# A graph layer pair on one core: four-tile chunks between the two edge passes

## What is computed

```python
# layer 0
h_mean = segment_sum(x[src], dst) / maximum(deg, 1)
out1   = batch_norm(x @ W_self1 + h_mean @ W_neigh1)          # over the nodes
h_max  = where(deg > 0, segment_max(relu(x @ W_pool + b_pool)[src], dst), 0)
out2   = batch_norm(x @ W_self2 + h_max @ W_neigh2)
x1     = layernorm(x + leaky_relu(out1 + out2, 0.01))         # over the features
# layer 1: 8 heads of 12
Q, K, V = x1 @ Wq + bq, x1 @ Wk + bk, x1 @ Wv + bv
score  = exp(clip(sum(K[src] * Q[dst] / sqrt(12) * (edge_attr @ We + be), heads), -5, 5))
out    = layernorm(x1 + segment_sum(V[src] * score, dst) / (segment_sum(score, dst) + 1e-6))
```

## Time and profile before

| | us |
|---|---|
| median of 3 runs | 4208.73 (4200.21 to 4212.95) |
| the profiled execution | 4194.81 |
| its span, first to last instruction | 4193.1 |

### The profile page before, as it was taken

How to read it: one execution, slowest core, us unless ns; L and a number is a source line. 1 busy time by engine, 2 the same in 40 slices (tenths; PEclk the granted TensorE clock), 3 DMA queues, 4 the chain that set the end, 5 groups by cost and what they waited for, 6 DMA issues and landing times.

```text
span 4193.1 us, 106504 instructions
## 1 busy us (share of the span) xinstructions
PE 3764.5 (90%) x30408; PEld 3251.6 (78%) x30408; DVE 2323.7 (55%) x5891; ACT 1500.0 (36%) x4201; POOL 3080.6 (73%) x3253
## 2 busy tenths in 40 slices
PE   7988888888888888888899999999999999999996
PEld 6777777777777777777678888888888888888885
DVE  6555555555555555555645555555555555555556
ACT  3333333333333333333433333333333333333333
POOL 7777777777777777777367777777777777777774
PEclk9999999999999999999889999999999999999997
DMA  3111111111111111111134444444444444444442
GB/s 92 40 39 39 39 39 39 39 39 39 39 39 39 39 39 39 39 39 39 41 114 120 118 118 118 118 118 118 118 118 118 117 118 117 119 117 118 118 118 74
DMA packets 208678, 330.89 MB, mean 79 GB/s; under 512 B 72878, under 2 KB 156521, under 8 KB 208649
## 3 DMA queue, kind: packets, MB, share of 16 engines
q0 software_dynamic: 129040, 238.05, 23.0%
q1 hardware_dynamic: 79608, 92.48, 7.5%
HBM read 323.08 MB, written 7.22 MB: 79 GB/s over the span
## 4 chain that ended last, share of the span: by engine, by line
POOL 42%; issue 33%; DMA 10%; PE 9%; DVE 5%; POOLq 1%; ACT 1%; DVEq 0%; ACTq 0%; SPq 0%
POOL kvg L413 42%; DMA kvg<-kv_table,idx 8%; DMA kvg<-in_x_dram,idx 2%; DVE prod L927 1%; DVE msg L951 1%; PE bank L1206 1%; PE bank L1041 1%; PE bank L1220 1%; PE bank L1052 1%; PE bank L1237 1%; PE bank L1215 1%; PE bank L1101 1%; PE bank L1084 1%; DVE S L661 1%; POOLq L408 0%
## 5 line engine op out<-in xcount | busy, mean ns | idle before, releaser
L413 POOL DMA_INDIRECT kvg<-kv_table,idx x1613 | 1525.3, 946 | 508.6 <-issue 465.0
L413 POOL DMA_INDIRECT kvg<-in_x_dram,idx x1613 | 1527.3, 947 | 496.9 <-issue 487.1
L678 DVE TENSOR_TENSOR_SCAN scan<-keepC,scan,bank 96x512 f32<-96x512 bf16 x404 | 515.4, 1276 | 493.9 <-PE bank L1052 489.6
L1041 PE MATMUL bank<-ident,kvg 128*96 128x128 f32 x3232 | 450.7, 283 | 225.6 <-DMA kvg<-in_x_dram,idx 215.7
L1041 PEld LDWEIGHTS bank<-ident,kvg 128*96 128x96 f32 x3232 | 365.7, 164 | 290.0 <-DMA kvg<-in_x_dram,idx 217.6
L1206 PE MATMUL bank<-ident,S 128*64 128x128 f32 x3232 | 433.6, 278 | 135.6 <-DVE S L661 133.2
L920 DVE TENSOR_TENSOR prod<-kvg,bank 128x384 f32<-128x384 f32 x404 | 223.8, 554 | 578.6 <-DMA kvg<-kv_table,idx 430.6
L1206 PEld LDWEIGHTS bank<-ident,S 128*64 128x64 f32 x3232 | 345.4, 137 | 224.2 <-issue 224.2
L1101 PEld LDWEIGHTS bank<-S,scanE 128*96 128x96 f32 x3232 | 340.4, 166 | 217.9 <-issue 214.7
L492 ACT COPY scanE<-bank 128x384 f32<-128x384 f32 x404 | 193.3, 478 | 753.1 <-PE bank L1093 753.1
L1220 PE MATMUL bank<-qwin,scan 64*128 64x96 f32 x3232 | 458.7, 283 | 0.0
(11 more groups left out here) (155 smaller groups left out, 5102.4 us busy)
## 6 DMA issues: line engine op xcount, KB each, us to landing
ea<-in_edge_attr_dram SPq DMA_DIRECT2D x402, 192.0 KB
kvg<-in_x_dram,idx POOLq DMA_INDIRECT x1613, 2.5
kvg<-kv_table,idx POOLq DMA_INDIRECT x1613
kv_table<-stage SPq DMA_DIRECT2D x6, 672.0 KB, 3.3
xN<-in_x_dram SPq DMA_DIRECT2D x6, 336.0 KB, 3.1
out_dram<-xN SPq DMA_DIRECT2D x6, 336.0 KB
src_all<-in_src_groups_dram SPq DMA_DIRECT2D x1, 804.0 KB
stage<-in_dst_groups_dram SPq DMA_DIRECT2D x1, 804.0 KB
```

The costliest lines, as they stand in the source:

```text
L413: pool.indirect_dma_start(out=to[:, r, j, :], out_offset=None, in_=table, in_offset=bass.IndirectOffsetOnAxis(ap=idx[:, r, j:j + 1], axis= ...
L678: dve.tensor_tensor_scan(out=scan[:, r % 2, :], data0=keepC[:, r % 2, :], data1=bank[2 + r % 2][0:D, :], initial=scan[:, (r + 1) % 2, GE - ...
L1041: pe.matmul(bank[0][0:D, j:GE:J], xg[:, r, j, 0:D], ident[:, :], start=True, stop=True)
```

## The change

Constants: LATE 3 to 2, so 99 strips and 112 rest columns; chunks of Q = 4 tiles, 13 of them, the last of one tile; HEAD = 12 turns.

- **Strips.** The four groups of a turn now do: count and reciprocal; mean; branch 1; branch 2 (before: count; reciprocal with branch 2; mean; branch 1).
- **Batch-norm statistics.** The statistics of the first 96 strips are aggregated ahead: branch 1 after turn 99, branch 2 after turn 100, on DVE between the turns (`gathered_stats`). What is left for later are 27 numbers a branch.
- **Rest columns.** Their count, reciprocal and mean move into the drain of pass 1 (`rest_out`), and so does the load of the flag.
- **Chunks.** Scaling and adding both branches is done by PE with two diagonal weight matrices; ACT makes the two parts of the leaky slope from PSUM, POOL adds them and then adds xT.
- **Table.** K and V are computed from the rows before normalising, with weights centred over the features (`w_kvc`), and DVE scales by the reciprocal deviation and adds the bias (`b_kv`) on the way to `stage`. It no longer waits for the normalised rows.
- **Turning back.** The normalised tiles are turned to `xT` one per group in the first 12 turns of pass 2 (PE, then DVE in `queries`), only the first tile before it; ACT clears `acc` one tile per group instead of POOL's one memset. ACT's `window(r)` waits for `s_qc` of group r - 1.
- **Warming.** Six pairs ahead of the chunks instead of nine; none within the chunks and in pass 2.

The diff, cut to its core:

```diff
-LATE = 3
+LATE = 2
+FLAG_TURN = 4
+NA = TURNS - LATE - 3
+Q = 4
+NQ = -(-NT // Q)
+HEAD = 12
...
+        def two_parts(eng, turn, lag, peel=0):
+            peel = max(peel, -(-lag // R))
+            for p in range(peel):
+                turn(p, range(R), lambda r: p * R + r >= 0, True)
+            if peel < HEAD:
+                with eng.Fori(peel, HEAD) as i:
+                    turn(i, range(R), lambda r: True, True)
+            with eng.Fori(HEAD, TURNS) as i:
+                turn(i, range(R), lambda r: True, False)
+            turn(TURNS, range(lag), lambda r: r < 0, False)
...
@@ sync (SP)
+            for k in range(NQ):
+                n = len(tiles_of(k))
+                sp.wait_ge(s_kvD, k + 1)
+                sp.dma_start(kv_table[k * Q * P:(k * Q + n) * P, :].rearrange("(t p) c -> p t c", p=P),
+                             stage[:, k * Q:k * Q + n, :]).then_inc(s_kvtab, 16)
...
@@ gpsimd (POOL)
+            for k in range(NQ + 1):
+                if k < NQ:
+                    u = acc[0:D, 1, columns(k)]
+                    pool.wait_ge(s_l, k + 1)
+                    pool.tensor_tensor(u, u, scan[:, k % 2, 0:u.shape[1]], ALU.add).then_inc(s_leak, 1)
+                if k >= 1:
+                    at = columns(k - 1)
+                    pool.wait_ge(s_leak, k)
+                    pool.tensor_tensor(acc[0:D, 0, at], acc[0:D, 1, at], xT[0:D, at], ALU.add).then_inc(s_h, 1)
-            pool.wait_ge(s_hN, NK)
-            pool.memset(acc[:, 0, :], 0.0).then_inc(s_free0, 1)
...
@@ scalar (ACT)
+            for k in range(NQ + 2):
+                if k < NQ:
+                    at = columns(k)
+                    act.wait_ge(s_u, k + 1)
+                    z = bank[k % 2][0:D, 0:at.stop - at.start]
+                    wait_past(act, s_leak, k - 1)
+                    act.activation(scan[:, k % 2, 0:at.stop - at.start], z, ACT.Identity, bias=shs[:, 1:2], scale=0.01)
+                    act.activation(acc[0:D, 1, at], z, ACT.Relu, bias=shs[:, 0:1], scale=0.99).then_inc(s_l, 1)
+                if k >= 2:
+                    t = k - 2
...
+                    act.wait_ge(s_mv, t + 1)
+                    act.activation(qr[b][:, 0:n], qmv[b].rearrange("p (n c) -> p n c", c=2)[:, 0:n, 1], ACT.Sqrt,
+                                   bias=eps_col[:, 0:1]).then_inc(s_sd, 1)
+                    act.wait_ge(s_nb, t + 1)
+                    for j in tiles_of(t):
+                        last = act.activation(xN[:, t * Q + j, :], bank[2 + b][:, j * D:(j + 1) * D], ACT.Identity,
+                                              bias=qb[b][:, j:j + 1], scale=qr[b][:, j:j + 1])
+                    last.then_inc(s_x1, 1)
...
                 def window(r):
+                    act.wait_ge(s_qc, freed(i, r, 1))
                     act.wait_ge(s_q, freed(i, r, 2))
...
@@ vector (DVE)
+                def rest_out():
+                    dve.wait_ge(s_countR, 1)
+                    dve.tensor_scalar_max(share_rest, bank[6][0:D, W:W + REST], 1.0).then_inc(s_shareR, 1)
...
+                    if isinstance(i, int) and i == TURNS and r == 1:
+                        rest_out()
+                        held["flag"] = load_flag(dve)
...
+            def gathered_stats(m, done, n):
+                part = stats[:, m, NA - 1, :]
+                dve.bn_aggr(mv[:, m, :], stats[:, m, 0:NA, :].rearrange("p n c -> p (n c)")).then_inc(done, 1)
...
+            pipeline(dve, turn1, 4, peel=XTURNS + 1, between=(count_descents, count_outside, count_early, centring),
+                     ending=(lambda: gathered_stats(0, s_part, 0), lambda: gathered_stats(1, s_part, 2)))
...
+            for k in range(NQ + 1):
+                if k < NQ:
...
+                    for j in tiles_of(k):
+                        last = dve.bn_stats(st[:, j, :], bank[2 + b][:, j * D:(j + 1) * D])
...
+                        last = dve.bn_aggr(mean_var[:, j, :], st[:, j, :])
...
+                if k >= 1:
+                    t = k - 1
+                    dve.wait_ge(s_kv, t + 1)
+                    for j in tiles_of(t):
+                        last = dve.scalar_tensor_tensor(
+                            out=stage[:, t * Q + j, :],
+                            in0=bank[4 + t % 2 * 2 + j // 2][:, j % 2 * 2 * D:(j % 2 + 1) * 2 * D],
+                            scalar=qr[t % 2][:, j:j + 1], in1=b_kv[:, :], op0=ALU.mult, op1=ALU.add)
+                    last.then_inc(s_kvD, 1)
+                if k < NQ:
+                    dve.wait_ge(s_sd, k + 1)
+                    dve.reciprocal(qr[b][:, 0:n], qr[b][:, 0:n]).then_inc(s_rs, 1)
+                    dve.wait_ge(s_rs, k + 1)
+                    dve.scalar_tensor_tensor(out=qb[b][:, 0:n], in0=mean_var[:, 0:n, 0], scalar=-1.0,
+                                             in1=qr[b][:, 0:n], op0=ALU.mult, op1=ALU.mult).then_inc(s_nb, 1)
...
@@ tensor (PE)
+                    if isinstance(i, int) and i == TURNS and r == 1:
+                        pe.wait_ge(s_acc, NG + AHEAD)
+                        pe.matmul(bank[6][0:D, W:W + REST], pick[:, :], acc[0:DSUM, 0, rest], start=True, stop=True
+                                  ).then_inc(s_countR, 1)
+                        held["flag"] = load_flag(pe)
...
-            stay_warm(9, 7)
+            for _ in range(6):
+                pe.matmul(bank[7][:, 0:CH], ident[0:D, :], xT[0:D, 0:CH], start=True, stop=True)
+            pe.wait_ge(s_diag, 2)
+            for k in range(NQ + 2):
+                if k < NQ:
...
+                    pe.matmul(o, diag[:, 0, :], acc[0:D, 0, at], start=True, stop=False)
+                    pe.matmul(o, diag[:, 1, :], acc[0:D, 1, at], start=False, stop=True).then_inc(s_u, 1)
+                if k >= 2:
+                    t = k - 2
+                    b = t % 2
+                    pe.wait_ge(s_h, t + 1)
+                    wait_past(pe, s_x1, t - 1)
+                    for j in tiles_of(t):
+                        last = pe.transpose(bank[2 + b][:, j * D:(j + 1) * D],
+                                            acc[0:D, 0, (t * Q + j) * P:(t * Q + j + 1) * P], ident[0:D, 0:D])
+                    last.then_inc(s_hN, 1)
+                    wait_past(pe, s_kvD, t - 1)
+                    pe.wait_ge(s_wkc, 1)
+                    for j in tiles_of(t):
+                        last = pe.matmul(bank[4 + b * 2 + j // 2][:, j % 2 * 2 * D:(j % 2 + 1) * 2 * D],
+                                         acc[0:D, 0, (t * Q + j) * P:(t * Q + j + 1) * P], w_kvc[:, :],
+                                         start=True, stop=True)
+                    last.then_inc(s_kv, 1)
...
-            pipeline(pe, turn2, 3)
+            two_parts(pe, turn2, 3, peel=HEAD)
```

More of the change, by code:

```diff
@@ L228, in wait_past, with pipeline @@
                 eng.wait_ge(s, value)
-        def pipeline(eng, turn, lag, turns=TURNS, per=R, peel=0, between=()):
+        def pipeline(eng, turn, lag, turns=TURNS, per=R, peel=0, between=(), ending=()):
             peel = max(peel, -(-lag // per))
@@ L238, in pipeline, with tiles_of, columns @@
                     work()
-            if peel < turns:
-                with eng.Fori(peel, turns) as i:
+            last = turns - len(ending)
+            if peel < last:
+                with eng.Fori(peel, last) as i:
                     turn(i, range(per), lambda r: True)
+            for p in range(last, turns):
+                turn(p, range(per), lambda r: True)
+                ending[p - last]()
             turn(turns, range(lag), lambda r: r < 0)
-        def node_rows(t, k):
-            return bank[t % 2 * 2 + k // 4][:, (k % 4) * D:(k % 4 + 1) * D]
+        def two_parts(eng, turn, lag, peel=0):
[8 more added lines that the diff above has]
+            turn(TURNS, range(lag), lambda r: r < 0, False)
+        def tiles_of(k):
+            return range(min(Q, NT - k * Q))
+        def columns(k):
+            return slice(k * Q * P, min((k + 1) * Q, NT) * P)
         def own_tiles(i, r):
@@ L461, in _, with clear @@
             last_residual()
+        def clear(act, at):
+            act.copy(acc[0:DMSG, 0, at], eps_col[0:DMSG, 1:2].to_broadcast([DMSG, P]))
         def copy_indices(act, i, r, s_done, s_i):
@@ L472, in _ @@
             act.wait_ge(s_ones, 2)
-            act.copy(warm[:, :], ones_col[0:1, :])
+            act.activation(warm[:, :], ones_col[0:1, :], ACT.Sqrt)
             act.wait_ge(s_src, 48)
@@ L508, in _ @@
             act.wait_ge(s_bn, 1)
             act.activation(std[:, :], mv[:, :, 1], ACT.Sqrt, bias=eps_col[0:D, 0:1]).then_inc(s_std, 1)
+            act.copy(acc[0:D, 1, rest], bank[0][0:D, 0:REST]).then_inc(s_copyR, 1)
             act.wait_ge(s_z, 1)
[L511 to L531 removed]
@@ L757, in _ @@
             dve.wait_ge(s_scan, NG + AHEAD)
-            with irregular(dve):
+            with dve.If(held["flag"] > 0):
                 with dve.Fori(0, NCH) as c:
@@ L1117, in turn1 @@
                         back(r - 2)
```

(17 more changed lines are left out.)

326 lines of the change are left out of this document (150 added, 176 removed).

## The result

The changed kernel took a median of 4214.68 us (4206.38 to 4226.14, 20 runs) against 4205.72 us for the kernel before (4200.21 to 4218.31, 20 runs, the three shown above among them): a ratio of 1.0019, 95% interval 1.0012 to 1.0026, so 8.0 us more (5.0 to 10.9). The profiled execution has a span of 4206.7 us, 13.6 more than the one before.

The account below looks back on a forecast made before the run. POOL's gathers bound both passes, so only its 91.9 us gap and a few stalls behind could move. Terms 4.8 - 3.4 + 4.2 - 2 = +3.6 gave 4212 us on the median; 8-in-10 range 4194 to 4228.

Parts of the forecast that it names:

- the four pieces: POOL's 91.9 us gap between passes: drain of pass 1, batch-norm constants, chunks, then 3.5 us to the first gather.
- Drain, +4.8: End of pass 1: second aggregation ahead of group 402's scan +2.5, mean of the last 112 columns +2.3; bounds +1 to +8.
- Constants, -3.4: Batch-norm constants, 12.1 us before: shorter aggregations and moved work -7.9, warming matmuls ahead of the first diagonal matmul +4.5.
- The term of the six pairs: Warming matmuls ahead of the first diagonal matmul: some 6.6 us, 2 beside the constants, so +4.5 (2.5 to 7.7).
- Chunks, +4.2, stage 63.5: Stage up to the last table row, 59.3 us before: 61.2 to 72, middle 63.5 taken, bounds 55 to 72.
- The ring: In the chunks, the written order makes a closed loop of waits over two chunks: about 8.8 us, 4.4 per chunk.
- The lock on the bias: In the chunks, DVE's bias operation waits about 1.2 us behind POOL's addition in every other chunk: stage 66.
- Start of pass 2, -2: Removing three warming pairs makes PE less late and recovers stalls of 3.7 us; -2 taken, bounds -3.7 to +4.
- The passes, 0: Both passes stay at POOL's 5.0 us per group; a transpose adds about 0.14 us to PE's 4.61: no cost.
- PE binds: Rival in the chunks: PE's matmuls set the pace, 3.5 us per chunk, stage 51.3, total 4195 us; chance 0.17.
- Table rows wait behind POOL: Rival in the chunks: DVE's table rows also wait for POOL, two waits of 1.2 us, stage 72, 4223 us; chance 0.14.
- The low clock: Rival in the chunks: PE falls to 0.50, 7.0 to 7.6 us per chunk, 4242 us in all; chance 0.07.

Follow-up runs that it names:

- e5: The changed kernel with both aggregations of the strips' statistics one turn earlier; ratio 1.0022 to the kernel before.
- e10: The changed kernel with the mean of the last 112 columns and the flag's load put back behind the drain; ratio 1.0009 to the kernel before.
- e2: The changed kernel with mean and variance of a chunk's rows in PSUM, so the bias reads only one SBUF operand; ratio 1.0006 to the kernel before.
- e8: The kernel before the change, without its three pairs of warming matmuls at the start of pass 2; ratio 0.9996 to the kernel before.
- b2: b1 without the six pairs of warming matmuls ahead of the chunks; ratio 0.9968 to the kernel before.
- e9: The changed kernel with pass 2's turns issued as transposes instead of matmuls by the identity; ratio 1.0023 to the kernel before.
- b1: The changed kernel with the edits of e1, e2 and e9 together; ratio 0.9974 to the kernel before.
- e1: The changed kernel with POOL adding a chunk's residual right behind that chunk's leak, not behind the next one's; ratio 0.9988 to the kernel before.

## Why the prediction held

It said 4212 us, within 0.3%, and 4214.7 and 1.0019 came; worked from the traces its sum of +3.6 stands against 6.5 for the same terms, and 8.0 (5.0 to 10.9) in the times. That the time lies as near as 2.7 us is in part luck: the sum was added to the median of three runs, 4208.7, and 20 runs gave 4205.7 for the same kernel, on which it would have said 4209. The likeliest case was the one that happened, but one term was missed, and one was right in its sum and wrong in its parts.

- **What bounds it, and the four pieces**: right. The gap and the head of pass 2 hold what the change did; elsewhere the passes keep 1.25 us per gather. The signs came as named: a gap near 97 (98.4), gathers 1.25 us apart at once, transposes 3.9 to 5.2 us apart (4.7 on the mean), POOL idle 2.67 us for ACT before a leak, ACT 2.06 for the bias, the last window addition 4.7 later. So did two that I had named against me: stalls in pass 2 beyond three groups, and a low clock in the stage, for some 18 of its 64 us.
- **Drain, +4.8**: measured +4.2 in this execution, +2.7 to +4.7 over the kernels with that code. The sum was right, its split was not. The block of the aggregation was put at +2.5 because the scan of group 402 had only 0.48 us to give; but the scan behind it had more, and the end moved by a few tenths (e5). The mean of the rest, put at +2.3 (the terms as listed add to 2.0), costs some 3 (e10). About 1 us lies ahead of the last scan, and its cause stays open.
- **Constants, -3.4**: measured -2.6. The term of the six pairs was undersized: they took 7.67 us where I took 6.6 (by the row of the nine pairs it would have been 6.0), and held the first diagonal matmul back by 5.3 (2052.8 to 2058.1) where I took 4.5, inside its bounds of 2.5 to 7.7.
- **Chunks, +4.2, stage 63.5**: measured 64.3 (64.3 to 65.7 over five kernels). The ring is the one written down, step for step. It takes 9.1 to 9.25 us, and 8.5 without the lock (e2), where I wrote 8.8 (the terms as listed add to 8.9 to 9.5). The lock on the bias is there in ten of the chunks, for 0.6 to 0.8 us in nine of them, not in every other one for 1.2. The Trainium skill, page "SBUF — State Buffer", "Who interferes with whom", had said that a VectorE instruction with two SBUF inputs contends with a GpSimd instruction that reads SBUF, and that one with at most one SBUF input, outside the two-port modes, does not. Both halves show: the bias takes 0.74 to 0.96 beside an addition in those nine and 0.16 once its mean lies in PSUM (e2); the table rows, with one of their two large inputs in PSUM, take 0.34 each in the ring's turn shown above, beside POOL's additions.
- **Start of pass 2, -2**: the stalls went whole, -3.7, its lower bound. The clock was low for the first 9.3 us of pass 2, and from 5.9 to 29.8 us before; that the warming pairs made the difference is argued, not shown (e8, b2).
- **The passes, 0**: this step failed. It priced a turn at 0.14 us of PE, as a transpose and with no row beside it, and found PE's period safely under 5.0. The change issues the turn as an fp32 matmul by the identity: two instructions, 0.53 us of the period, 5.14 in all. A transpose would have been 0.39, not 0.14, and the period 5.00, with no cover left either (e9, b1, b2). The text had named what stood behind the cover (48 x 0.15 = 7 us) and took 0. 48 x 0.14 = 6.7, less PE's lead, is what came: 3.7 here, 0.3 to 5.9 elsewhere. It hid in the result because the two stall terms cancel.
- **Rivals.** "PE binds": not with this order; e1 made it true with one moved addition. "Table rows wait behind POOL": no, four rows take 1.36 us in every chunk. "The low clock": in parts of the stage only, where a turn of the ring took 10.3 us instead of 9.1 to 9.25, never through it.

## What to carry over

A written order over several engines is a ring: list its steps with their operands' engines, and ask which step may be moved behind the hand-over, before asking which engine is busiest; here one POOL addition moved by one place was worth 12 us of the gap, more than the 8.0 that the whole change cost. When a step is moved under cover of a loop with a fixed pace, price it from a row of the very instruction in such a loop (a transpose added 0.39 us here, a matmul by the identity 0.53, and 0.14 had been assumed) and set the new period, not the added time, against the pace. Two terms that cancel, as the stalls that went and those that came, look in the total like none.

## What the runs showed of the hardware that I had not expected

- A turn of a 128x96 fp32 tile is two instructions and 0.46 us as a matmul by the identity, one and 0.31 as a transpose (e9). Between other matmuls it adds 0.53 and 0.39 us to PE's period.
- The lock between DVE and POOL is lifted by the place of one small operand: 0.74 to 0.96 us became 0.16 (e2).
- A gather that lands 4.8 us late near the end lets PE idle for 3.6 us; its clock falls to 0.50 and stays there for 20 us, in which PE has no further idle time, and POOL loses 4.3 us although PE's period at full clock, 4.61, is under 5.0.
- The pace of the gathers itself differs between executions: from start to start 1.248 to 1.249 us in pass 1 of some profiles, 1.251 in others, and the last gather of pass 1 ended at 2027.4 to 2031.2 us in kernels with the same pass 1. Spans of single profiles are no measure for less than 5 us; the gap is a better one, but it too came to 91.9 and 95.3 us with the same code.
